# A six-stage perceiver block: mixture entry rebuilt, other beginning, row-outer outputs, packed tables

## What is computed

```python
x = x + _L0_xattn_ref(_layernorm(x), ctx_1024, ctx_1024)     # gelu(x @ ctx_e.T) @ ctx_e over 8192 context rows
x = x + _L0_attn_ref(_layernorm(x), ...)                      # in-projection, causal conv, selective scan, gate, out
x = x + _L0_ffn_ref(_layernorm(x), ...)                       # bit-linear, conv of 3, silu, bit-linear
x = x + _L1_xattn_ref(ctx_1024, _layernorm(x), ...)           # 8 heads, keys from the context and x
x = x + _L1_attn_ref(_layernorm(x), ...)                      # 16 heads, attention over channels (64 x 64)
x = x + _L1_ffn_ref(_layernorm(x), ...)                       # mixture, below

# _L1_ffn_ref, T = 512 rows, E = 8 experts, top 2, capacity 80
xn = xf * rsqrt(mean(xf * xf) + eps);  probs = softmax(xn @ router_w.T)
topk_p, topk_i = top_k(probs, 2);      rw = topk_p / sum(topk_p)
dispatch = argsort(~sel, stable)[:, :capacity];  xg = xf[dispatch]
eout = (silu(xg @ rg) * (xg @ ru)) @ rd
routed = zeros.at[dispatch].add(eout * w * valid);  shared = silu(x @ sg) * (x @ su) @ sd
return shared + routed
```

## Time and profile before

| | |
|---|---|
| median of 3 runs (lowest, highest) | 2605.74 us (2596.19, 2606.24) |
| profiled execution | 2607.39 us, its span 2605.7 us |
| PE busy | 2451.6 us, 94% of the span |
| DVE, ACT, POOL busy | 1866.5, 1176.3, 591.0 us |
| mean granted TensorE clock | 0.968 of full speed |
| output sums complete: stage 1, stage 4, stage 5 | 397, 1846, 1988 us |

### The profile page before, as it was taken

How to read it: one execution, slowest core, us unless ns; L and a number is a source line. 1 busy time by engine, 2 the same in 40 slices (tenths; PEclk the granted TensorE clock), 3 DMA queues, 4 the chain that set the end, 5 groups by cost and what they waited for, 6 DMA issues and landing times.

```text
span 2605.7 us, 33056 instructions
## 1 busy us (share of the span) xinstructions
PE 2451.6 (94%) x11394; PEld 1669.0 (64%) x11394; DVE 1866.5 (72%) x1944; ACT 1176.3 (45%) x1428; POOL 591.0 (23%) x406
## 2 busy tenths in 40 slices
PE   6999998998776999999999999999897999999998
PEld 5777877754343777777764555554675777777775
DVE  5868855399988577777788887887444766666654
ACT  2333422376444433343326666664333545545553
POOL 3655544298942211111110000000000000000000
PEclk9999998999977999999999999999798999999999
DMA  7677754722021455455524553553112366666653
GB/s 275 235 234 257 266 164 156 289 73 81 0 97 49 156 201 209 193 218 227 206 108 163 182 182 111 182 182 118 48 61 122 124 228 228 216 230 228 227 218 134
DMA packets 140017, 447.99 MB, mean 172 GB/s; under 512 B 24656, under 2 KB 55068, under 8 KB 105488
## 3 DMA queue, kind: packets, MB, share of 16 engines
q1 hardware_dynamic: 111360, 380.04, 40.8%
q10 hardware_dynamic: 28560, 66.66, 7.3%
HBM read 326.94 MB, written 119.71 MB: 171 GB/s over the span
## 4 chain that ended last, share of the span: by engine, by line
PE 47%; DVE 2%; DMA 1%; ACT 1%; issue 0%; SPq 0%; POOL 0%; DVEq 0%; ACTq 0%
PE ps L2688 9%; PE ps L2269 9%; PE ps L2270 9%; PE ps L2271 9%; PE ps L2664 8%; PE ps L2946 1%; PE ps L2571 1%; DMA sh_raw<-in_s_parts 0%; DVE peak L1948 0%; PE ps L2972 0%; PE ps L2777 0%; PE ps L2910 0%; PE ps L2756 0%; PE ps L2743 0%; PE ps L2781 0%
## 5 line engine op out<-in xcount | busy, mean ns | idle before, releaser
L2016 DVE TENSOR_TENSOR sums<-sums,pT 128x1024 f32<-128x1024 f32 x272 | 313.6, 1222 | 61.9 <-ACT pT L1476 60.8
L1948 DVE SCALAR_TENSOR_TENSOR peak<-ps,rs_all,peak 128x1024 f32<-128x1024 f32 x214 | 263.7, 1278 | 47.9 <-PE ps L2571 47.5
L1476 ACT ACTIVATE pT<-ps,rs_all 128x1024 f32<-128x1024 f32 x214 | 219.9, 1123 | 169.8 <-PE ps L2664 169.8
L2688 PE MATMUL ps<-pT,values 128*64 128x512 f32 x1088 | 242.5, 596 | 0.0
L2688 PEld LDWEIGHTS ps<-pT,values 128*64 128x64 f32 x1088 | 74.5, 137 | 146.5 <-issue 118.6
L1092 POOL TENSOR_TENSOR cT_lo<-cT_raw,cT_hi 128x512 fp32r<-128x512 f32 x60 | 78.3, 1305 | 378.6 <-ACT cT_hi L1386 378.6
L2386 PE MATMUL ps<-work,ident 128*128 128x512 f32 x256 | 128.5, 632 | 31.0 <-POOL work L1023 15.6
L2156 DVE TENSOR_TENSOR rgu_lo<-rgu_raw,rgu_hi 128x2048 fp32r<-128x2048 f32 x64 | 143.9, 2289 | 5.1 <-ACT rgu_hi L1566 5.1
L985 POOL TENSOR_TENSOR ctx_lo<-ctx_raw,ctx_hi 128x512 fp32r<-128x512 f32 x64 | 104.6, 1635 | 129.4 <-DVE ctx_hi L1689 129.4
L1942 DVE TENSOR_TENSOR peak<-kept_rows,peak 128x1024 f32<-128x1024 f32 x58 | 68.6, 1222 | 77.3 <-ACT kept_rows L1404 77.3
L1784 DVE TENSOR_TENSOR_SCAN ps<-ps,work 128x1024 f32<-128x1024 f32 x51 | 116.6, 2286 | 7.6 <-ACT ps L1309 7.6
(11 more groups left out here) (488 smaller groups left out, 6660.5 us busy)
## 6 DMA issues: line engine op xcount, KB each, us to landing
rgu_raw<-in_r_gate_up SPq DMA_DIRECT2D x64, 1024.0 KB, 4.8
rd_raw<-in_r_down SPq DMA_DIRECT2D x32, 1024.0 KB, 4.8
kept_rows_dram<-kept_rows SPq DMA_DIRECT2D x29, 1024.0 KB, 3.9
kept_back<-kept_rows_dram SPq DMA_DIRECT2D x29, 1024.0 KB, 6.7
sh_raw<-in_s_parts SPq DMA_DIRECT2D x32, 768.0 KB, 4.3
key_rows<-key_hi SPq DMA_DIRECT2D x17, 1024.0 KB, 3.9
key_rows<-key_lo SPq DMA_DIRECT2D x17, 1024.0 KB, 5.9
value_rows<-values SPq DMA_DIRECT2D x17, 1024.0 KB, 8.0
```

Source lines behind the costliest of these rows:

```text
L1476: nc.scalar.activation(pT[:, i], ps[:, b:b + 2], ACT.Exp, scale=rs_all[:, bass.ds(c * KT + attend_tile(j, i)[1], 1)]).then_inc(s4_exp.sem, 1)
L1948: nc.vector.scalar_tensor_tensor(peak[:, p], ps[:, b:b + 2], rs_all[:, bass.ds(c * KT + kt, 1)], peak[:, p], ALU.mult, ALU.max).then_inc(s ...
L2016: nc.vector.tensor_tensor(sums[:, p], sums[:, p], pT[:, i], ALU.add).then_inc(s4_sum.sem, 1)
L2688: done = nc.tensor.matmul(ps[e * DK:(e + 1) * DK, 6 + p], values[:, s, kt, h * DK:(h + 1) * DK], pT[:, i, e], start=start and kt == 0, sto ...
```

## The change

It does the following. (1) Stage 1: ACT issues the four w1 loads after its first context chunk's high part; DVE makes that chunk's low part ahead of xT_lo; the first product waits for each part of xT_lo by itself and goes to bank 0. Stage 2's first unit does the same. (2) The fourteen small tables are packed on the host into two, of 184 and 124 floats for each of 128 partitions; the router's weights, already transposed, are in the second, and are split before stage 5. (3) Stage 4's output product and the second half of stage 5's run row tile by row tile. (4) Stage 5: the first half of wo5 is split while the last value units run, and the shared expert's first weights are loaded and split between the output pairs; tiles are placed anew in SBUF so that these lie over nothing in use. (5) Stage 6: constants are made in stage 5; row squares, xn_hi and xn_lo are made before the router; the pairwise comparison is three operations on 256 elements; the counting is four fp32r matmuls; the gather comes right behind dispatch; shared_down and the second shared up-product are cut in quarters and laid between the return transposes, which ACT alone copies out; the first routed weights are loaded earlier.

The diff, cut to what the text speaks of and with less indentation (new places of tiles and the host's packing are left out):

```diff
-STREAM_BANK = {**{("x", n): 2 + n % 2 for n in range(IB)}, ("bc", 0): 3, **{("wx", n): 2 + n % 2 for n in range(IB)},
+STREAM_BANK = {**{("x", n): 2 + n % 2 if n else 0 for n in range(IB)}, ("bc", 0): 3, **{("wx", n): 2 + n % 2 for n in range(IB)},
@@ sync
+sp.dma_start(scan_small[:], a["scan_small"]).then_inc(small_loaded, 16)
+sp.dma_start(late_small[:], a["late_small"]).then_inc(small_loaded, 16)
...
-sp.wait_ge(*s5_x(TT))
-sp.dma_start(router_w[0:NE], a["L1_ffn_router_w"]).then_inc(rw_loaded.sem, 16)
...
+sp.wait_ge(*p5_mm(UNITS))
+sp.wait_ge(*w5_lo(3 * XCB + 2))
 for j in range(2):
     load_shared(0, j)
+sp.wait_ge(*o5_mm(XPAIRS))
+for j in range(2):
     load_expert(0, j, 0)
     load_expert(0, j, 1)
+sp.wait_ge(*s5_x(TT))
+for j in range(2):
     load_rows(0, j)
 sp.wait_ge(*s_down(1))
 load_shared(0, 2)
@@ gpsimd (before ln_scales(5) instead of behind it)
+link(pool, nc.gpsimd.memset(counts[:].bitcast(F32), 1.0))
+nc.gpsimd.affine_select(out=before, in_=before.bitcast(F32), compare_op=ALU.is_gt, fill=0.0, base=0,
+                        pattern=[[1, P]], channel_multiplier=-1).then_inc(counts_made.sem, 1)
+link(pool, nc.gpsimd.memset(earlier[:], 1.0))
+nc.gpsimd.affine_select(out=earlier[:], in_=earlier[:], compare_op=ALU.is_gt, fill=0.0, base=0,
+                        pattern=[[1, NE], [-1, NE]], channel_multiplier=0).then_inc(counts_made.sem, 1)
@@ scalar
-for c in range(W_CHUNKS):
-    load_weights(0, c)
-ln_evacuate(0)
...
 s1_front(0, 0)
+for c in range(W_CHUNKS):
+    load_weights(0, c)
+ln_evacuate(0)
 for n in range(CHUNKS):
...
+nc.scalar.activation(rwT_hi[:], router_wT, ACT.Copy).then_inc(rw_hi.sem, 1)
...
-act_e.wait_ge(*wo5_loaded(16))
-act_e.wait_ge(*p5_mm(UNITS))
-for half in range(2):
-    four = slice(half * 4, half * 4 + 4)
-    nc.scalar.activation(wo5_hi[:, four], wo5_raw[:, four], ACT.Copy).then_inc(w5_hi.sem, 1)
-    for p in range(half * 4, half * 4 + 4):
-        act_e.wait_ge(*o5_mm(p + 1))
-        nc.scalar.activation(o5_hi_t[:, p], ps[:, p % 4], ACT.Copy).then_inc(o5_hi.sem, 1)
...
-act_e.wait_ge(*s5_x(TT))
...
+        if c == 3 * XCB - 1 and j == 0:
+            act_e.wait_ge(*wo5_loaded(16))
+            act_e.wait_ge(*s5_sim(2))
+            out_hi(0)
...
-ln_evacuate(3)
-act_e.wait_ge(*rw_T(1))
-nc.scalar.activation(rwT_hi[:], ps[:, 3, 0:DT * NE], ACT.Copy).then_inc(rw_hi.sem, 1)
-shared_hi(0, 0)
...
+for p in range(4):
+    pair_hi(p)
+out_hi(1)
+for p in range(4, XPAIRS):
+    pair_hi(p)
+    if p in (4, 5):
+        shared_hi(0, p - 4)
...
+for tt in range(TT - 1):
+    row_squares(tt)
+    row_hi(tt)
+ln_evacuate(3)
+row_squares(TT - 1)
+row_hi(TT - 1)
 act_e.wait_ge(*m_wide(1))
-nc.scalar.activation(wide[0:NE], ps[0:NE, 1], ACT.Copy).then_inc(m_wide_out.sem, 1)
-shared_hi(0, 1)
+nc.scalar.activation(wide[0:NE], ps[0:NE, 0], ACT.Copy).then_inc(m_wide_out.sem, 1)
...
 shared_gate(0)
-for tt in range(TT):
-    nc.scalar.activation(xn_hi[:, tt], xn[:, tt], ACT.Copy).then_inc(x6_hi.sem, 1)
+act_e.wait_ge(*m_mask(1))
+expert_hi(0, 0, 0)
 shared_act_hi(0)
 shared_gate(1)
-expert_hi(0, 0, 0)
-expert_hi(0, 0, 1)
-shared_act_hi(1)
-shared_hi(0, 2)
 for n in range(2 * DT):
...
-for e in range(1, NE, 2):
...
+for e in range(4):
+    return_out(e)
+act_e.wait_ge(*m_disp(1))
+expert_hi(0, 0, 1)
+for e in range(4, NE):
+    return_out(e)
+shared_act_hi(1)
+shared_hi(0, 2)
 rows_hi6(0, 0)
@@ vector
 ln_rows(0, lambda tt: None)
+dve.wait_ge(s1_cThi, 1)
+nc.vector.tensor_tensor(ctxT_lo[:, 0], ctxT_raw[:, 0, 0], ctxT_hi[:, 0].bitcast(F32), ALU.subtract).then_inc(s1_cTlo, 1)
 ln_low(0)
...
+    if n == 0:
+        return
...
+dve.wait_ge(*rw_hi(1))
+nc.vector.tensor_tensor(rwT_lo[:], router_wT, rwT_hi[:].bitcast(F32), ALU.subtract).then_inc(rw_lo.sem, 1)
...
+            out_lo(0)
...
-ln_rows(5, add_fifth)
...
-dve.wait_ge(*m_iota(1))
-link(dve, nc.vector.tensor_scalar(place1[:], ps[:, 0, 0:CAP], 1.0, None, ALU.add))
-shared_lo(0, 0)
-shared_lo(1, 1)
+for p in range(4):
+    pair_lo(p)
+out_lo(1)
+for p in range(4, XPAIRS):
+    pair_lo(p)
+    if p in (4, 5):
+        shared_lo(p - 4, p - 4)
+
...
+for tt in range(TT):
+    dve.wait_ge(*s5_out(tt + 1))
+    nc.vector.tensor_tensor(x_res[:, tt], ps[:, 4 + tt], x_res[:, tt], ALU.add).then_inc(s5_x.sem, 1)
+    dve.wait_ge(*s5_x(tt + 1))
+    ln_measure(tt, x_res)
+    if tt:
+        ln_row(5 * TT + tt - 1, tt - 1, x_res)
+    if tt >= 2:
+        row_low(tt - 2)
+ln_row(5 * TT + TT - 1, TT - 1, x_res)
+row_low(TT - 2)
+ln_low(3)
+row_low(TT - 1)
...
+dve.wait_ge(*m_iota(1))
+link(dve, nc.vector.tensor_scalar(place1[:], ps[:, 3, 0:CAP], 1.0, None, ALU.add))
...
-for tt in range(TT):
-    each, other = (probs6[:, tt].unsqueeze(k).to_broadcast([P, NE, NE]) for k in (2, 1))
-    nc.vector.tensor_tensor(above[:, tt], other, each, ALU.is_gt)
-    link(dve, nc.vector.tensor_tensor(equal[:, tt], other, each, ALU.is_equal))
-    link(dve, nc.vector.tensor_tensor(equal[:, tt], equal[:, tt], earlier[:], ALU.mult))
+each, other = (probs6[:].unsqueeze(k).to_broadcast(ties) for k in (3, 2))
+nc.vector.tensor_tensor(above[:], other, each, ALU.is_gt)
+link(dve, nc.vector.tensor_tensor(equal[:], other, each, ALU.is_equal))
+link(dve, nc.vector.tensor_tensor(equal[:], equal[:], earlier[:].unsqueeze(1).to_broadcast(ties), ALU.mult))
...
-shared_act(0, 1)
...
-shared_act_lo(0)
...
                         ALU.is_equal).then_inc(m_disp.sem, 1)
-for tt in range(TT):
-    dve.wait_ge(*x6_hi(tt + 1))
...
-shared_act(1, 1)
-expert_lo(0, 0, 0)
-shared_act_lo(1)
-for n in range(2 * DT):
+shared_act(0, 1)
+
...
-for e in range(0, NE, 2):
-    dve.wait_ge(*m_rT(e + 1))
...
+for n in range(2 * DT - 2):
+    gathered_low(n)
+shared_act_lo(0)
+for n in (2 * DT - 2, 2 * DT - 1):
+    gathered_low(n)
+expert_lo(0, 0, 0)
 expert_lo(0, 0, 1)
+shared_act(1, 1)
+shared_act_lo(1)
 shared_lo(2, 2)
 rows_lo6(0, 0)
@@ tensor
-pe.wait_ge(xT_lo_ready, DT)
...
     for dt in range(DT):
-        last = product(ps[:, 2 + m % 2], (ctxT_hi[:, m % 2, dt], ctxT_lo[:, m % 2, dt]),
+        if first:
+            pe.wait_ge(xT_lo_ready, dt + 1)
+        last = product(ps[:, 0 if first else 2 + m % 2], (ctxT_hi[:, m % 2, dt], ctxT_lo[:, m % 2, dt]),
...
+s1_up(0, 0, first=True)
...
-pe.wait_ge(xT_lo_ready, 2 * DT)
...
     for kt in range(4):
+        if place == 0:
+            pe.wait_ge(xT_lo_ready, DT + kt + 1)
         unit_product(place, kt)
...
-for p in range(PAIRS):
-    pe.wait_ge(*o_lo(p + 1))
-    for tt in range(TT):
-        t = slice(tt * P, (tt + 1) * P)
+for tt in range(TT):
+    t = slice(tt * P, (tt + 1) * P)
+    for p in range(PAIRS):
+        if tt == 0:
+            pe.wait_ge(*o_lo(p + 1))
         done = product(ps[:, 4 + tt], (xT_hi[:, p, t], xT_lo[:, p, t]), (wout_hi[:, p], wout_lo[:, p]), p == 0, p == PAIRS - 1)
...
+    return product(ps[:, 4 + tt], (o5_hi_t[:, p, t], o5_lo_t[:, p, t]), (wo5_hi[:, p], wo5_lo[:, p]),
...
+pe.wait_ge(*w5_lo(3 * XCB + 1))
+for p in range(4):
     pe.wait_ge(*o5_lo(p + 1))
     for tt in range(TT):
...
+        rows_out(p, tt)
+    weigh_rows(p + 4)
+pe.wait_ge(*w5_lo(3 * XCB + 2))
+for tt in range(TT):
+    for p in range(4, XPAIRS):
+        if tt == 0:
+            pe.wait_ge(*o5_lo(p + 1))
+        done = rows_out(p, tt)
+    done.then_inc(s5_out.sem, 1)
...
-pe.wait_ge(xT_lo_ready, 4 * DT)
-pe.wait_ge(*rw_loaded(16))
-for dt in range(DT):
-    done = nc.tensor.transpose(ps[:, 3, dt * NE:(dt + 1) * NE], router_w[0:NE, dt * P:(dt + 1) * P], ident[0:NE, 0:NE])
-done.then_inc(rw_T.sem, 1)
...
 pe.wait_ge(*rw_lo(1))
 for dt in range(DT):
     e_ = slice(dt * NE, (dt + 1) * NE)
-    done = product(ps[0:NE, 1], (rwT_hi[:, e_], rwT_lo[:, e_]), (xT_hi[:, dt], xT_lo[:, dt]), dt == 0, dt == DT - 1)
+    pe.wait_ge(xT_lo_ready, 3 * DT + dt + 1)
+    done = product(ps[0:NE, 0], (rwT_hi[:, e_], rwT_lo[:, e_]), (xT_hi[:, dt], xT_lo[:, dt]), dt == 0, dt == DT - 1)
...
-def shared_up(n, j, i, bank):
-
-    for dt in range(DT):
+def shared_up(n, j, i, bank, parts=range(DT)):
+
+    for dt in parts:
...
+    if parts[-1] == DT - 1:
+        done.then_inc((s_g, s_u)[i].sem, 1)
+
+def shared_down_rows(n, j, tt, first=False):
+    t = slice(tt * P, (tt + 1) * P)
+    return product(ps[:, 4 + tt], (s_act_hi[:, t], s_act_lo[:, t]), (sh_hi_t[:, j % 2, 2], sh_lo_t[:, j % 2, 2]), first, False)
+
+def shared_down(n, j):
...
 pe.wait_ge(*sh_lo(1))
-shared_up(0, 0, 0, 2)
+shared_up(0, 0, 0, 2, range(1))
+pe.wait_ge(*counts_made(2))
+nc.tensor.matmul(ps[:, 3, 0:CAP], all_before, before[:, 0:CAP], start=True, stop=True).then_inc(m_iota.sem, 1)
...
 done.then_inc(m_logits.sem, 1)
+shared_up(0, 0, 0, 2, range(1, DT))
 shared_up(0, 0, 1, 1)
 pe.wait_ge(*m_mask(1))
-for tt in range(TT):
-    for k in range(tt + 1):
-        done = nc.tensor.matmul(ps[:, 0, 128 + tt * NE:128 + (tt + 1) * NE], before[:] if k == tt else ones[:], mask6[:, k],
-                                start=k == 0, stop=k == tt)
```

(19 more changed lines are left out.)

201 lines of the change are left out of this document (88 added, 113 removed).

## The result

| | before | after |
|---|---|---|
| median (all executions), us | 2605.99 (2596.19 to 2607.61) | 2557.68 (2557.04 to 2566.67) |
| ratio | | 0.9835, 95% interval 0.9811 to 0.9860 |
| span of the profiled execution, us | 2605.7 | 2556.2 |
| PE busy, us | 2451.6 | 2439.5 |
| DMA packets under 512 B | 24656 | 11784 |

A forecast was written before the change was run, and what follows sets the result against it. PE streams without a gap nearly everywhere, so each edit was costed as microseconds of PE's start moved: 13.0 + 7.7 + 1.8 + 3.2 + 20.9 = 46.6; 2607.4 less 46.6 is 2560.8, stated as 2560 us, range 2546 to 2582.

The forecast's parts named there:

- beginning: Kernel start: x lands earlier with weight loads issued later, and PE needs only the first low half; 13.0 us, ends 9 and 14.
- packed tables: Stage 1's loop near 360: fourteen small loads delay a store ACT awaits; hole and slow passes go, 7.7 us, ends 0 and 8.
- second stage's entry: Start of stage 2: PE waits for one low half instead of all four; 1.8 us, ends 0 and 1.8.
- output order, cross attention: Stage 4's output: row-outer order finishes three rows earlier, so the fourth add comes sooner; 3.2 us, ends 2 and 3.4.
- ties and positions: Router: ties in three operations on 256 elements gain 1.2 us; positions in 4 fp32r passes gain 3.2, ends 2 and 3.6.
- dispatch, gather, to the experts: Mixture: gathering starts with dispatch, 7.2 us earlier, while shared products move between return transposes; net 4.5 us, ends 2 and 6.
- the shared splits' landing: Attention's output: shared weights' splits wait for loads, making o_lo of pair 6 late for PE; cost 1.0 us, ends 0 and 5.
- rival (b): Attention's output and experts: sh_hi waits for an 11 us landing, PE idles 5 us, ACT evictions cost more; 2571 us, chance 0.08.
- (a): Rival on stage 1's loop: the late store is not due to the small loads, the hole at 375 stays; 2568 us, chance 0.07.
- (c): Rival on the beginning: x lands late whatever is queued, gain 3 us from single waits alone; 2570 us, chance 0.05.
- (d): Rival on the experts' loop: each of 32 turns waits for a 1.9 us split, +61 us; 2621 us, chance 0.02.
- the attention's split: Stage 5: splitting half the output weights early removes a 2.79 us hole and slow passes but delays Exp 1.25; net 3.2 us.

The follow-up runs named there:

- b_loads_late: The kernel before with only the four first weight loads issued behind the first context block's high part; median 2590.27 us, ratio 0.9942 to before.
- b_packed: The kernel before with only the fourteen small tables loaded as two packed ones, other tiles at their old addresses; median 2594.97 us, ratio 0.9961.
- a_pairs_outer: The changed kernel with both output products back in the old order, pairs outside and rows inside; median 2572.55 us, ratio 0.9858 to before.
- a_low_late: The changed kernel with xn's four low halves made behind the dispatch matrix instead of ahead of the router; median 2570.05 us, ratio 0.9864 to before.
- a_exp_first: The changed kernel with the first half of the output weights' high split on ACT behind Exp; median 2562.76 us, ratio 0.9831 to before.
- b_place64: The kernel before with 64 bytes left free ahead of x_res, so x_res, xn, xT_hi and xT_lo lie higher; median 2611.14 us, ratio 1.0027.

## Why the prediction was right, point by point

Shifts below are starts before minus starts after; each row of the table is the growth of the shift over its stretch, so the last column adds up to the 49.5 between the spans (49.6 as rounded here).

| step | predicted | measured |
|---|---|---|
| beginning (27.95 to 14.89) | 13.0 | 13.1 |
| packed tables (the hole and its slow passes) | 7.7 | 7.7 |
| rest of stage 1's loop | 0 | +1.8 |
| second stage's entry | 1.8 | 1.8 |
| from there to stage 4's output | 0 | +1.4 |
| output order, cross attention | 3.2 | 2.8 |
| from there to the comparison of queries and keys | 0 | +2.6 |
| attention's splits, shared splits, output order, to the fourth add | 3.2 - 1.0 + 3.5 = 5.7 | 4.8 |
| fourth add to router | 2.8 | 2.7 |
| router to logits | 3.5 | 4.0 |
| ties and positions | 4.4 | 4.5 |
| dispatch, gather, to the experts | 4.5 | 5.5 |
| experts' loop | 0 | -3.1 |
| **sum** | **46.6** | **49.5** |

**Right, and shown by a run**: the beginning (b_loads_late), the tables (b_packed), the output orders (a_pairs_outer, 3.7 and 3.5) and the low halves beside POOL's multiply (a_low_late). The 7.7 of the tables holds for the execution it was read from; others with the same loads had a smaller hole. The entry, the router (5.6 us to the logits, 6.1 forecast), the ties and the positions are shown by the trace of the changed kernel alone. So is the shared splits' landing: ACT waited 5.06 us for it and PE 0.34, where I had charged 1.0; rival (b), with 5 us, did not come:

```profile
1945.76 0.50 PE L2301 MATMUL ps<-wo_hi,o_lo 128*128 128x512 f32 x1 [0.34 <-DVE o_lo L2130]
```

**The rivals.** (a) falls with b_packed and (c) with b_loads_late. (d) did not come either: PE's waits in the experts' loop are the same in both kernels (four, 3.7 us in all, in the last expert's turns), and the loop's 3 us are pace. From the gather to the experts were 19.6 us, forecast 20.8.

**The step that failed is the attention's split**, forecast at 3.2 and measured at 1.9. The hole of 2.79 and the slow passes behind it did go, and the delay of Exp was sized about right: 1.25 was charged, and PE's wait ahead of the attention matrix grew by 1.08, from 1.34 to 2.42. What the sum lacks is the clock behind that wait: PE fell to the 1.2 GHz level, and 1.6 us of slow passes came back one unit earlier. Up to the first output pass the gain is 0.2, and with the passes behind it 1.9. a_exp_first, with the wait at 1.26 and no slow passes, gains 2.7 more. The 1.6 came in five of six executions with such a wait; in a_pairs_outer's they didn't. The page's rule on a switch of tables (the Trainium skill, "ScalarE: Activation LUTs", What ACT_TABLE_LOAD costs) was rightly not used: the load at 1916.85 takes 1.28 and Exp starts at 1918.14, with no draining between.

**The reason given for the tables was half wrong.** "PE idles at none of the others" is not true of the kernel before: late stores made PE wait three more times. That the tables caused the big hole is shown; that stage 1's loop had slack otherwise is not so.

**What is missing from the sum cancels nearly.** x's tiles moved by 64 bytes, because I read the packed table as a matter of loads and not of addresses: 5.5 us in stage 1's loop (122 groups by 0.045) and 3.1 in the experts'. Against them stand 7.3 us in stage 1's loop (its 1.8 and those 5.5) of waits, mostly for stores, and slow passes that the execution before had and this one had not, and 4.0 us between stages 2 and 5 in stretches that nothing in the change was meant to speed up. Of these, 2.6 go with the granted clock in stage 5 (0.95 against 0.90), why, no run shows; the other 1.4 stay open, and stage 2 alone took 326 to 332 us in the fourteen executions. That the median came within 3 us of the forecast is in part luck: 8.6 us of a cost that was not thought of met 11.3 us of gain that was not either, and the 7.3 of stage 1 differ from execution to execution: the changed kernel's second profiled execution has lost 4.2 of them.

## What to carry over

Where PE idles at the start of a kernel, look at what else is in flight while the first operand lands: 4 MB issued beside 1 MB cost it 9.8 us. A wait on a slack engine (here ACT for a store) that is covered in most turns is still a bound: take it away with a buffer before trusting that a faster loop will be faster. When a change resizes a lasting tile, everything allocated behind it moves; compare the start-to-start time of unchanged passes before and after, for the place of PE's operands alone was worth some 7 us here (b_place64). And before a difference in one profiled execution is put down to an edit, compare the granted clock of that stretch, and look at a second execution.

## What the hardware showed that was not expected

- Passes of 128x512 that read xT_hi and xT_lo went at 0.227 us each at one place, 0.230 at 64 bytes more and 0.233 at 128 bytes more, at the same granted clock of 1.00 (twelve in 2.72, 2.76 and 2.79).
- A wait of 1.1 to 1.34 us for the attention matrix left PE at the 2.4 GHz level in eight executions of eight. After one of 2.3 to 2.5 it fell for eight passes (0.42 each) in five of six, and in one, with 2.42, it did not.
- With the same 309 passes and PE busy throughout, one stretch took 70.0 to 74.9 us, as the granted clock was 0.95 to 0.88.
- One subtraction on DVE with two SBUF operands took 4.96 us beside a POOL multiply of 4.85, its three neighbours 0.68.
